# Mixture-of-experts stage in eight streams with conditional weight loads, row scatter of the results, and a combine of plain loads with sums on TensorE

## The reference, cut to what matters

```python
x  = u                                         # 4096 tokens (4 x 1024) of 256 channels, f32
xn = layernorm(x)
x  = x + state_space(xn) + moe(xn)             # moe: 64 experts, 6 chosen for each token, plus a shared expert
x2 = x + attention_1(layernorm(x)) + ffn(layernorm(x))   # per token: softmax over 64 channels of 16 heads; gated FFN
# moe, routed part:
h      = silu(xn @ eg_w[e].T) * (xn @ eu_w[e].T)         # 128 wide, for each expert e
routed = sum over the 6 chosen e of  weight(token, e) * (h @ ed_w[e].T)
```

## Time and profile before

| | |
|---|---|
| median of 3 runs | 4280.25 us |
| the profiled execution | 4279.34 us |
| its span, first to last instruction | 4277.6 us |
| PE / DVE / ACT / POOL busy | 86% / 78% / 46% / 83% of the span |
| DMA | 291.38 MB, 154902 packets |
| mean granted TensorE clock | 0.938 |

### The profile page before, as it was taken

The page is one execution under the profiler, slowest core; times in us unless marked ns, Lnnn a source line. Parts: engine busy times, 40 slices in busy tenths (PEclk is TensorE's granted clock), DMA queues, the critical chain, the costliest instruction groups (busy, mean ns, idle before and its releaser), DMA issues.

```text
span 4277.6 us, 78411 instructions
## 1 busy us (share of the span) xinstructions
PE 3659.8 (86%) x27585; PEld 3249.3 (76%) x27777; DVE 3339.0 (78%) x3764; ACT 1976.5 (46%) x2564; POOL 3559.3 (83%) x1937
## 2 busy tenths in 40 slices
PE   4275999910189999999999999999999999999999
PEld 3143888810078888888888888888888888888888
DVE  8644343446489888899889888898889888899887
ACT  1010333300055555555555555555555555555555
POOL 1675555567599999999999999999999999999997
PEclk8687999955599999999999999999999999999999
DMA  9122999954300000000000000000000000000000
GB/s 367 70 101 70 384 385 385 384 190 127 106 3 5 5 5 5 5 6 6 7 5 5 5 5 5 5 6 5 7 5 5 5 5 5 5 5 6 5 8 5
DMA packets 154902, 291.38 MB, mean 68 GB/s; under 512 B 22608, under 2 KB 116048, under 8 KB 154576
## 3 DMA queue, kind: packets, MB, share of 16 engines
q0 software_dynamic: 38912, 151.04, 9.7%
q1 hardware_dynamic: 115664, 135.80, 9.0%
HBM read 181.77 MB, written 104.99 MB: 67 GB/s over the span
## 4 chain that ended last, share of the span: by engine, by line
POOL 39%; issue 29%; PE 3%; DVE 1%; ACT 0%; POOLq 0%; another core or an unknown queue 0%; ACTq 0%; DVEq 0%
POOL at_s L1109 34%; POOL at_m L1093 2%; POOL at_fall L1089 2%; POOL at_m L1086 1%; PE at_den L1325 1%; PE at_num L1325 1%; PE at_work L1297 0%; DVE at_pv L1225 0%; DVE at_s L1217 0%; POOLq L1108 0%; PE at_work L1302 0%; PE at_misc L1355 0%; ACT at_s L1180 0%; PE at_work L1313 0%
## 5 line engine op out<-in xcount | busy, mean ns | idle before, releaser
L1109 POOL TENSOR_TENSOR at_s<-at_s,at_m 128x2048 f32<-128x2048 f32 (+15 forms) x1024 | 2549.5, 2529 | 115.9 <-DVE at_s L1217 114.6
L1180 ACT ACTIVATE at_s<-at_s 128x2048 f32<-128x2048 f32 (+15 forms) x1024 | 1135.8, 1112 | 1259.2 <-POOL at_s L1109 1253.6
L1217 DVE TENSOR_TENSOR at_s<-at_q,at_kp 128x2048 f32<-128x2048 f32 (+15 forms) x1024 | 1309.2, 1279 | 318.6 <-PE at_den L1325 301.9
L1325 PE MATMUL at_den<-k_ident,at_s 128*128 128x128 f32 x10240 | 1290.8, 273 | 55.4 <-ACT at_s L1180 55.4
L1225 DVE TENSOR_TENSOR at_pv<-at_s,at_vp 128x2048 f32<-128x2048 f32 (+15 forms) x1024 | 1309.7, 1279 | 21.2 <-issue 10.0
L1325 PE MATMUL at_num<-k_ident,at_pv 128*128 128x128 f32 x10240 | 1286.2, 273 | 10.1
L1325 PEld LDWEIGHTS at_num<-k_ident,at_pv 128*128 128x128 f32 x10240 | 1162.2, 141 | 145.4 <-issue 123.1
L1325 PEld LDWEIGHTS at_den<-k_ident,at_s 128*128 128x128 f32 x10240 | 1156.9, 141 | 79.9 <-ACT at_s L1180 61.9
L674 POOL DMA_INDIRECT moe_w<-experts,e_weight_row x256 | 242.1, 946 | 213.5 <-PE moe_yp L701 173.2
L138 POOL DMA_INDIRECT slot_x<-e_xn,e_slot x192 | 209.0, 1088 | 152.1 <-DVE e_slot L358 87.6
L694 PE MATMUL moe_gu<-moe_xT,moe_w 128*128 128x128 f32 x2048 | 274.9, 277 | 13.9 <-DVE moe_xT L737 12.0
(11 more groups left out here) (219 smaller groups left out, 3262.8 us busy)
## 6 DMA issues: line engine op xcount, KB each, us to landing
slot_x<-k_region SPq DMA_DIRECT2D x16, 2048.0 KB, 23.3
moe_x<-slot_x SPq DMA_DIRECT2D x256, 128.0 KB
slot_out<-moe_yo SPq DMA_DIRECT2D x256, 128.0 KB
xT<-cmb_xT SPq DMA_DIRECT2D x33, 128.0 KB, 2.1
at_xT<-xT SPq DMA_DIRECT2D x33, 128.0 KB, 2.0
e_x<-u SPq DMA_DIRECT2D x4, 1024.0 KB, 10.5
moe_w<-experts,e_weight_row POOLq DMA_INDIRECT x256, 6.1
x<-e_x SPq DMA_DIRECT2D x4, 1024.0 KB, 5.6
```

Of the source, the lines that this page charges most:

```text
L1109: nc.gpsimd.tensor_tensor(part(s_all, c), part(s_all, c), by_query(m[h][:], c), ALU.subtract).then_inc(sub_done, 1)
L1180: nc.scalar.activation(part(s_all, c), part(s_all, c), ACT.Exp, scale=C ** -0.5).then_inc(exp_done, 1)
L1217: v.tensor_tensor(part(s_all, c), by_query(q[h][:], c), by_key(kp[:], c), ALU.mult).then_inc(mult_done, 1)
L1325: ins = nc.tensor.matmul(dst[:, b * P:(b + 1) * P], buf[:, at:at + P], k.ident[:], start=(x == 0 and b == 0), stop=False, is_transpose=Tru ...
```

## The change

The slot rows grow from 256 to 268 floats (ROW): behind each token's channels stand its six slot numbers (plus one) and six numbers from which the row of a choice in a token-major tensor can be worked out. Routing writes them with two more VectorE operations before the slot numbers are released. Instead of the table of weight rows it makes block_expert (the expert of each block) and fresh (1 where it is another expert than in the block before, or where a stream starts).

Experts: the ring of 8 buffers becomes 8 streams; buffer j takes blocks 32j to 32j+31, one in each of 32 turns. SP now issues the fetches of weights: it reads the expert and the flag of a block from SBUF into registers, and issues the fetch with the flag as its condition, so that weights stay in the buffer while the stream stays with its expert. With 64 experts and 8 streams at most 71 of 256 fetches move data. POOL works out, for four blocks at a time, the row of each slot (seven small operations, after one VectorE comparison), and scatters the results to these rows of the tensor picked (rows of padding go behind it), 256 indirect transfers. The stores of SP are gone.

Combine: a token tile's six rows now lie together, and one plain load of SP (768 KB) fetches them; the ring has 5 buffers. ScalarE makes five diagonal matrices of weights for each tile, TensorE multiplies them with five of the six result tiles and sums them in PSUM, VectorE adds the sixth and the sum. Groups are of 4 tiles. TensorE and ScalarE handle the transposition of tile n-7 in the step of tile n. ScalarE issues the stores to xT, VectorE's preparation of weights is cut into 8 steps.

```diff
 NSH = 2
 SLOT_BLOCKS = T * TOPK // P + E
 SLOTS = SLOT_BLOCKS * P
-FILLS, ZERO_ROW = 16, 1024
+ROW = D + 2 * TOPK
+STREAM = 32
+FILLS, ZERO_ROW = 16, 4 * ROW
...
                 c.join()
+                dve.wait_ge(tailed, 1)
+                c.mark(v.tensor_copy(k.xn[:, :, D:D + TOPK], top8[:, :, 0:TOPK]))
+                c.mark(v.tensor_tensor(k.xn[:, :, D + TOPK:ROW], tail_base[:], top8[:, :, 0:TOPK], ALU.subtract))
+                c.join()
                 v.tensor_scalar(k.slot[:], top8[:], -1.0, None, ALU.add).then_inc(slots_done, 1)
...
                 dve.wait_ge(bexp_done, 1)
-                v.tensor_scalar(k.weight_row[:], block_of, float(P),
-                                k.iota_p[:, 0:1], ALU.mult, ALU.add).then_inc(widx_done, 1)
+                c(v.tensor_copy(k.block_expert[:], block_of))
+                c(v.tensor_tensor(k.fresh[:, 1:], k.block_expert[:, 1:], k.block_expert[:, 0:SLOT_BLOCKS - 1],
+                                  ALU.not_equal))
+                v.memset(view(k.fresh[:], [[STREAM, SLOT_BLOCKS // STREAM]]), 1).then_inc(widx_done, 1)
...
-    RING = 8
-    TURNS = SLOT_BLOCKS // RING
+    RING, HALF_RING = SLOT_BLOCKS // STREAM, SLOT_BLOCKS // STREAM // 2
+    TURNS = STREAM
...
+        own = a.sb("own", [P, 2, RING])
+        hit, found = a.sb("hit", [P, RING, TOPK]), a.sb("found", [P, 2, RING])
+        row = a.sb("row", [P, 2, RING], I32)
...
-                for b in range(SLOT_BLOCKS):
-                    wait(pool, y_done, b - RING + 1)
-                    pool.indirect_dma_start(w[b % RING][:], None, weights,
-                                            bass.IndirectOffsetOnAxis(ap=k.weight_row[:, b:b + 1], axis=0)
-                                            ).then_inc(w_in[b % RING], 16)
...
+                for i in range(TURNS):
+                    for h in range(2):
+                        part = slice(h * HALF_RING, (h + 1) * HALF_RING)
+                        pool.wait_ge(hit_done, 2 * i + h + 1)
+                        nc.gpsimd.tensor_tensor(hit[:, part, :], hit[:, part, :], xr[:, part, D + TOPK:ROW], ALU.mult
+                                                ).then_inc(rows_known, 1)
+                        pool.wait_ge(rows_known, 2 * i + h + 1)
+                        c(nc.gpsimd.tensor_tensor(hit[:, part, 0:3], hit[:, part, 0:3], hit[:, part, 3:6], ALU.add))
+                        c.mark(nc.gpsimd.tensor_tensor(found[:, 0, part], hit[:, part, 0], hit[:, part, 1], ALU.add))
+                        c(nc.gpsimd.tensor_tensor(found[:, 1, part], hit[:, part, 2], own[:, 1, part], ALU.add))
+                        c(nc.gpsimd.tensor_tensor(found[:, 0, part], found[:, 0, part], found[:, 1, part], ALU.add))
+                        for j in range(h * HALF_RING, (h + 1) * HALF_RING):
+                            wait(pool, y_out[j], 16 * (i - 1))
+                        c.mark(nc.gpsimd.tensor_copy(row[:, i % 2, part], found[:, 0, part]))
+                        nc.gpsimd.tensor_scalar(own[:, :, part], own[:, :, part], float(P), None, ALU.add
+                                                ).then_inc(hit_free, 1)
+                        c.join()
+                        for j in range(h * HALF_RING, (h + 1) * HALF_RING):
+                            pool.wait_ge(y_ready, done(i, j))
+                            pool.indirect_dma_start(scratch["picked"],
+                                                    bass.IndirectOffsetOnAxis(ap=row[:, i % 2, j:j + 1], axis=0),
+                                                    yo[j][:], None).then_inc(y_out[j], 16)
+                for j in range(RING):
+                    pool.wait_ge(y_out[j], 16 * TURNS)
...
+                def find(i, h):
+                    part = slice(h * HALF_RING, (h + 1) * HALF_RING)
+                    if not isinstance(i, int):
+                        dve.wait_ge(hit_free, i * 2 + (h - 1))
+                    nc.vector.tensor_tensor(hit[:, part, :], xr[:, part, D:D + TOPK],
+                                            view(own[:, 0, part], [[1, HALF_RING], [0, TOPK]]), ALU.is_equal
+                                            ).then_inc(hit_done, 1)
...
                             nc.vector.tensor_copy(xT[j][:], tr[j % 2][:]).then_inc(xT_ready, 1)
+                        if j and j % HALF_RING == 0:
+                            find(i, j // HALF_RING - 1)
                         if j >= 1:
                             dve.wait_ge(gate_ready, done(i, j - 1))
...
-                blocks_of = lambda t: scratch[t].rearrange("(b p) d -> p b d", p=P)
...
+                x_rows = scratch["slot_x"].rearrange("(b p) d -> p b d", p=P)
+                w_rows = io["experts"].rearrange("(e p) d -> p e d", p=P)
+                def load_x(i, j):
+                    if not isinstance(i, int) or i:
+                        sp.wait_ge(turned, done(i, j) - RING)
+                        sp.wait_ge(rows_known, i * 2 + (j // HALF_RING - 1))
+                        settle(sp, sp_settled)
+                    sp.dma_start(xr[:, j:j + 1, :], x_rows[:, bass.ds(i + j * STREAM, 1), :]).then_inc(x_in[j], 16)
+                def load_w(i, j):
+                    wait(sp, y_done, done(i, j) - RING)
+                    at = bass.ds(i + j * STREAM, 1)
+                    expert = sp.value_load(k.block_expert[0:1, at], min_val=0, max_val=E - 1)
+                    fresh = sp.value_load(k.fresh[0:1, at], min_val=0, max_val=1)
+                    sp.dma_start(w[j][:].unsqueeze(1), w_rows[:, bass.ds(expert, 1), :], cond=fresh
+                                 ).then_inc(w_in[j], 16)
+                def turn_in(i):
                     for j in range(RING):
-                        load(i, j)
-                        store(i - 1, j)
...
+                        load_x(i, j)
+                        load_w(i, j)
+                block_loop(sp, turn_in)
...
-        RING, GROUP, LATE = 4, 8, 2
+        RING, TURN_RING, GROUP, LATE, DIAG = 5, 4, 4, 2, 5
+        AFTER = GROUP + LATE + 1
         y = [a.sb(f"y{j}", [P, TOPK, D]) for j in range(RING)]
+        diag = [a.sb(f"diag{i}", [P, DIAG, P]) for i in range(3)]
...
                 c = Chain(pool, pool_step)
-                def root(g):
+                for g in range(NT // GROUP):
                     pool.wait_ge(moments, (g + 1) * GROUP)
                     c(nc.gpsimd.tensor_scalar(rstd[:, members(g)], mv[:, members(g), 1], EPS, None, ALU.add))
                     nc.gpsimd.tensor_tensor(rstd[:, members(g)], rstd[:, members(g)], k.minus_half[:, members(g)],
                                             ALU.pow).then_inc(pow_done, 1)
-                for n in range(NT):
-                    wait(pool, summed, n - RING + 1)
...
+                def last_choice(n):
+                    dve.wait_ge(y_in[n % RING], 16 * (n // RING + 1))
+                    v.scalar_tensor_tensor(out=k.x[:, n, :], in0=y[n % RING][:, DIAG, :],
+                                           scalar=k.choice_w[:, DIAG, n:n + 1], in1=k.x[:, n, :],
+                                           op0=ALU.mult, op1=ALU.add).then_inc(first_done, 1)
...
+                last_choice(0)
                 for n in range(NT):
-                    dve.wait_ge(y_in[n % RING], 16 * TOPK * (n // RING + 1))
-                    for j in range(TOPK):
...
+                    if n + 1 < NT:
+                        last_choice(n + 1)
+                    dve.wait_ge(first_done, n + 1)
+                    dve.wait_ge(acc_done, n + 1)
+                    v.tensor_tensor(k.x[:, n, :], k.x[:, n, :], acc[n % 2][:, 0:D], ALU.add).then_inc(summed, 1)
                     dve.wait_ge(summed, n + 1)
                     c.mark(v.bn_stats(stats[:, n, :], k.x[:, n, :]))
                     if n % GROUP == GROUP - 1:
...
                             v.bn_aggr(mv[:, i, :], stats[:, i, :]).then_inc(moments, 1)
                     if n >= GROUP + LATE and (n - LATE) % GROUP == 0:
                         normalise((n - LATE) // GROUP - 1)
-                    if n == NT // 2 - 1:
-                        weights()
+                    if n >= NT // 4 and n % 2 == 1 and (n - NT // 4) // 2 < 8:
+                        weights((n - NT // 4) // 2)
...
-                for n in range(NT):
-                    pe.wait_ge(xn_done, n + 1)
...
+                for n in range(NT + AFTER):
+                    if n < NT:
+                        pe.wait_ge(y_in[n % RING], 16 * (n // RING + 1))
+                        pe.wait_ge(diag_ready, n + 1)
+                        wait(pe, summed, n - 1)
+                        for j in range(DIAG):
+                            ins = nc.tensor.matmul(acc[n % 2][:, 0:D], diag[n % 3][:, j, :], y[n % RING][:, j, :],
+                                                   start=(j == 0), stop=(j == DIAG - 1))
+                        ins.then_inc(acc_done, 1)
+                    if n >= AFTER:
+                        i = n - AFTER
+                        pe.wait_ge(xn_done, i + 1)
```

(38 more changed lines are left out.)

143 lines of the change are left out of this document (65 added, 78 removed).

## The result

The changed kernel takes 4474.41 us (median of 4 runs, 4468.11 to 4481.42), the kernel before 4280.21: ratio 1.0454, 95% interval 1.0435 to 1.0472. It is slower by 194 us, where I had forecast 100. The profiled execution took 4481.42 us, with a span of 4479.7.

A forecast was written before the change was run, and what follows sets the result against it. PE paced the experts and POOL's issue the combine; after the change SP would pace the experts. Routing +1, experts +175, last scatter +2 and combine -78 make +100 on 4279.34: 4380 us, slower, range 4213 to 4549.

The forecast's parts named there:

- Sign and bound: Whole kernel: slower, chance 0.62, because SP's (SyncE's) issues and register loads would pace the experts, +175 us.
- the forecast's own 4304 to 4457: Whole kernel: range in us for a register load of 0.2 to 0.5 us, chance 0.38; the full range was 4213 to 4549.
- L: Experts, SP: time of one register load, two per block, taken as 0.35 us; 0.05 us of it are 26 us.
- With it a block is 2.41 us: Experts, SP: a block's two issues, five sequencer steps and two register loads of 0.35 us take 2.41 us.
- five steps of 0.07: Experts, SP: five more sequencer steps a block at 0.07 us each, within 1.71 us a block before register loads.
- 256 of them 617 us: Experts: 256 blocks of 2.41 us on SP make the stage 617 us, +175 us.
- +2 us: Experts' end: the last scatter's issue and landing take the place of a plain store, +2 us.
- Rival A: Experts: register load cheap, 0.1 us or less, POOL the bound, +35 us; 4240 us in all, chance 0.34.
- 4508: Whole kernel in us by the Trainium skill's 600 ns load: a block 2.91 us, experts 745 us, +303.
- Each step is therefore a loop: Combine: ScalarE and TensorE wait for each other in each tile's step, 6.35 us; 24 steps 152 us, stage -78 us.
- the middle between the clock's two levels: Combine: a step is 5.25 us with the fast clock, 7.45 with the slow; the middle, 6.35, was taken.
- no line of them is touched, so they only start earlier or later: Attention and FFN, 3121.8 us: unchanged in length, put at 0 in the sum.

The follow-up runs named there:

- e3: Changed kernel with the inputs of four blocks fetched by one transfer: experts 628.1 us, 103 less.
- e5: Changed kernel with a third register load, with limits and unused, in each block: experts 844.6 us, 114 more.
- e6: Changed kernel with expert and flag in one number, read by one register load without limits: experts 582.1 us, 149 less.
- e4: Changed kernel with ScalarE's diagonals made one tile ahead in the combination: combination 125.7 us in place of 214.
- e9: Kernel before the change with 320 satisfied waits on TensorE at the combination's end: attention 3169.8 us in place of 3121.8, in all 4336.3 us.
- e7: Changed kernel with 64 satisfied waits on TensorE at the combination's end: attention 3117.2 us; the next run, with 128 waits, 3121.3 us.
- e12: Changed kernel with 256 satisfied waits on TensorE at the combination's end: attention 3118.1 us.

## Why the prediction was right and wrong

- **Sign and bound: right.** Slower, with SyncE's queue as the bound of the experts: shown by e3, e5 and e6, which moved the stage by what they took from or gave to that queue (-103, +114, -149 us), and by the records without a wait. The time lies in the range, but the change is 194 us where the forecast had 100, and 4474 is above the forecast's own 4304 to 4457. It would lie inside these without the 51 us of the attention, a stage put at nothing.
- **L: near, and its block right by luck.** "With it a block is 2.41 us", from L = 0.35. A load takes 0.30 us up to the next instruction, which by the prediction's own measure is 26 us of the stage, and the steady block is 2.39. The sum came out through errors that cancel. The two loads are 0.10 us less than counted. The second issue with its surroundings was put at 0.68 us and takes 0.28, since the issue of a transfer whose condition is false is 0.08 us, not 0.34, and 219 of the 256 are of that kind; 37 show 0.33, and the stage's traffic (126 GB/s over 664 us are 84 MB, of which inputs and outputs take 69) leaves room for 38 fetches of 393 KB. Against these stands what the limits and the address bring, 0.82 us a block, where the sum had five steps of 0.07, 0.35. The two "ISA" behind each load in the order of the change are such a comparison and its assertion: I had counted them, at the price of a plain step.
- **"256 of them 617 us": the term that failed**, by 32 us. From the first register load at 424.9 to the last weight issue at 1073.7 are 648.7 us, 2.53 a block. 37 issues that fetch are 0.25 us longer, 9 us; the turn's end costs SyncE some 0.5 us of branch and register steps 31 times, 16 us; 82 of the 512 loads take up to 0.78 us in place of 0.27 and add 15 us. With 256 x 2.39 = 612 that is 652, near enough. All three come once in some blocks, which a steady block doesn't show.
- **"+2 us" for the last scatter: mis-sized.** From the last weight issue to the combination's first load are 14.9 us, where the kernel before has 2.2 behind its last store: the last blocks' inputs still have to land and pass all engines, then come the row numbers of half a turn, four scatters and their landing.
- **Rival A and the Trainium skill's figure.** A had L at 0.1 or less, and the sign turns at 0.155; it is 0.30. The Trainium skill (DMA: Bandwidth & Descriptors, Latency and other measured facts) gives 600 ns as the floor; SyncE's load of one number shows 262 ns at the shortest here, so the measurement decides, and 4508 was too high by that term.
- **Combination: mechanism right, size off by 11 us.** "Each step is therefore a loop" is in the rows, and e4 shows that it was the bound. The step is 6.8 us and not 6.35: the middle between the clock's two levels was taken for the products, and they ran near the lower one in nearly every step, although the mean of a step is 0.75. 24 steps are 162.8 us where the sum has 152. The stage's start was 7 us longer than in the sum and its tail 8 us shorter, which cancel.
- **Attention: missing.** The prediction says of this stage that "no line of them is touched, so they only start earlier or later". That is the step that failed outright. No line was changed, but 672 more records on TensorE moved its loop to a bad place, +51 us. By the groups of turns above, a turn of 192.2 us becomes 193.8 with the second standstill alone, 194.2 with the lower clock alone, and 196.3 on average with both: 4.1 us, 57 in 14 turns. The kernel before had three turns of 194.2, 6 us, and the difference is the 51.

## What to carry to other kernels

Count what a queue carries instruction by instruction, with the limits, conditions and address steps that a dynamic value brings: here they cost as much as the loads, and one packed number without limits took 149 us off. Where a step makes something for the next one and then waits, put the making ahead of the wait: here a change of a few lines gave 89 us, part of it through the clock. And when an untouched loop of short instructions becomes slower, look at its turn's start for a standstill without a releaser and shift the stream by some tens of instructions before looking for a cause in the work.

## What the hardware showed unexpectedly

- A loop's jump costs TensorE one standstill of about 2 us or two, by the place of its start in blocks of 256 instructions, and behind the second the granted clock fell to its lower level in most turns (14 of 14 in the changed kernel, 12 of 14 in e9): 48 to 51 us in 15 turns (e7 to e9, e12).
- 64 waits in a row on one semaphore gave 32 records: two go into one.
- A register load is 262 to 268 ns on SyncE in most cases, 0.3 to 0.78 us in 82 of 512; a transfer whose condition is false holds the queue for 0.08 us, a true one for 0.33.
- Chips differ by 181 to 193 us for the same kernel, each measured at one time only. On the slower ones steps of SyncE that take 0.06 us elsewhere now and then take 0.7 us, and the changed kernel's stages before the experts are 150 us longer. Why wasn't tried.
